# A 16-slot hand-written schedule: first products taken inside the gelu blocks, softplus behind the second one

## What is computed

```python
x = x + 0.5 * ffn(layernorm(x))       # "f1": 8 experts, all computed, the gate's argmax picks one per token
x = x + mamba(layernorm(x))           # rmsnorm, in_proj, conv of 4 taps, silu, scan, gate, out_proj
x = x + 0.5 * ffn(layernorm(x))       # "f2"
# ffn:   h = gelu(x @ W1[e] + b1[e]) (exact gelu);  y = h @ W2[e] + b2[e]
# mamba: dt = softplus(dt_x @ dt_proj_w.T + dt_proj_b)
#        h = exp(dt * A) * h + (dt * x) * B;  y = sum_n h * C + D * x;  256 channels, 16 states each
```

## Time and profile before

| | us |
|---|---|
| median of 3 runs (1549.31 to 1573.08) | 1550.01 |
| the profiled execution, its own time | 1555.03 |
| its span, first to last instruction | 1553.2 |
| mean granted TensorE clock in it | 0.837 of 2.4 GHz |

### The profile page before, as it was taken

One profiled execution on the slowest core, in us unless ns is written; L12 is line 12 of the kernel. 1 busy time (PEld: TensorE's weight loads), 2 busy tenths in 40 slices (PEclk: granted clock), 3 DMA queues, 4 the chain that ended last, 5 costly groups with the idle time before them and its releaser, 6 DMA issues.

```text
span 1553.2 us, 16302 instructions
## 1 busy us (share of the span) xinstructions
PE 1254.8 (81%) x5188; PEld 613.9 (40%) x5188; DVE 1060.3 (68%) x1713; ACT 872.8 (56%) x1171; POOL 1066.0 (69%) x900
## 2 busy tenths in 40 slices
PE   3776858698988988898888988898888878767676
PEld 1333414244343434344343434344343435333343
DVE  2022878868777776768777776778777777979810
ACT  0245655574756657574756557574756566464422
POOL 1026788978586777778586777778586777988500
PEclk9978878798788879888888889898888888888776
DMA  3005141404032322214132322204132322232000
GB/s 81 1 0 198 38 161 42 157 28 161 25 118 79 117 89 103 89 26 173 29 121 76 118 88 91 101 26 173 26 115 78 113 86 104 95 110 88 5 3 14
DMA packets 60405, 130.02 MB, mean 84 GB/s; under 512 B 7744, under 2 KB 26864, under 8 KB 52128
## 3 DMA queue, kind: packets, MB, share of 16 engines
q1 hardware_dynamic: 60320, 128.98, 24.5%
HBM read 106.94 MB, written 22.02 MB: 83 GB/s over the span
## 4 chain that ended last, share of the span: by engine, by line
PE 42%; ACT 31%; DVE 16%; issue 7%; POOL 2%; SPq 1%; ACTq 0%; DMA 0%; DVEq 0%; POOLq 0%
PE PH L451 15%; PE G L440 8%; ACT dA L611 8%; PE PY L466 7%; ACT hs L592 7%; DVE dA L737 6%; PE PH L450 4%; ACT hs L585 4%; DVE hb L735 3%; PE G L520 3%; ACT L592 3%; DVE hb L741 3%; PE Y L478 3%; ACT L593 3%; DVE xs L754 2%
## 5 line engine op out<-in xcount | busy, mean ns | idle before, releaser
L914 POOL TENSOR_TENSOR hb<-dtx_rep,bs 128x1024 f32<-128x1024 f32 x256 | 597.6, 2355 | 0.0
L737 DVE TENSOR_TENSOR_SCAN dA<-dA,hb 128x512 f32<-128x512 f32 x352 | 429.5, 1220 | 62.3 <-ACT dA L611 55.5
L611 ACT ACTIVATE dA<-dt_rep,A 128x512 f32<-128x512 f32 x512 | 338.8, 688 | 147.8 <-DVE hb L741 138.3
L585 ACT COPY hs<-PH 128x512 f32<-128x512 f32 x256 | 149.5, 584 | 431.9 <-PE PH L451 431.6
L451 PE MATMUL PH<-xnT,W 128*128 128x512 f32 x512 | 360.9, 794 | 0.0
L466 PE MATMUL PY<-W,hs 128*128 128x128 f32 x2048 | 325.9, 308 | 0.0
L466 PEld LDWEIGHTS PY<-W,hs 128*128 128x128 f32 x2048 | 282.8, 211 | 100.0 <-issue 88.1
L922 POOL TENSOR_TENSOR hb<-hb,cs 128x1024 f32<-128x1024 f32 x80 | 188.3, 2354 | 186.5 <-DVE hb L735 186.5
L735 DVE TENSOR_TENSOR_SCAN hb<-dA,hb 128x512 f32<-128x512 f32 x160 | 186.9, 1210 | 150.1 <-ACT dA L611 146.1
L741 DVE TENSOR_TENSOR hb<-dA,cs 128x512 f32<-128x512 f32 x352 | 243.5, 692 | 25.2 <-DVE dA L737 0.9
L478 PE MATMUL Y<-hb,Sel 128*32 128x512 f32 x1024 | 168.4, 733 | 16.0 <-DVE hb L741 8.6
(11 more groups left out here) (85 smaller groups left out, 1171.5 us busy)
## 6 DMA issues: line engine op xcount, KB each, us to landing
dtx_rep<-dtx_rows SPq DMA_DIRECT2D x32, 1024.0 KB, 6.6
dt_rep<-dt_rows SPq DMA_DIRECT2D x32, 1024.0 KB, 7.6
bs<-bc_rows SPq DMA_DIRECT2D x64, 256.0 KB, 3.7
...
```

The source lines that it names most:

```text
L585: nc.scalar.copy(hs[:, w, e, :], PH[:, :]).then_inc(ph_free, 1)
L611: nc.scalar.activation(dA[u % NA][:, :], dt_rep[:, h, g, :], ACT.Exp, scale=A[:, h, g, q:q + 1]).then_inc(decay, 1)
L737: nc.vector.tensor_tensor_scan(a, a, x_in_hb, 0.0, ALU.mult, ALU.add).then_inc(scan, 1)
L914: nc.gpsimd.tensor_tensor(hb[:, s % HR], dtx_rep[:, h, 2 * m:2 * m + 2, :], bs[:, q, None, :].broadcast_to([P, 2, CH]), ALU.mult).then_inc ...
```

## The change

Of f2's eight first products, experts 0, 1 and 2 move from slots 1, 2 and 3 of a lap to slot 15 of the lap before; the other five stand in slots 1, 2, 3, 5, 6. f1's experts 0 and 1 stand at the ends of slots 8 and 9 instead of in 9 and 10. A first product and its copy now have places of their own: ACT copies f1's expert 0 between the two gelus of f2's block (slot 7.5), and f2's expert 2 between the two gelus of f1's block (slot 15.5); the copies of slot 15 stand one ahead of the first and one between the two decays. f2's last two second products stand between those first products. softplus moves on ACT from slot 7 to 9.5, behind f2's gelu block and the copy of ln_f2; on POOL dt moves from 8.0 to 9.5 and dt*x from 8.5 to 10.0, and SP's stores of both and its first two fetches from slot 9 to 11. The last sum of the scan moves from slot 1 to slot 0, the output projection and DVE's addition of it one place and one slot earlier, f2's statistics from 6.0 to 5.0, and `gate_f2` behind the first product of slot 10.

```diff
-W1_AT = [[(s, k, 3) for s, k in ((9, 0), (10, 0), (11, 0), (12, 0), (12, 1), (13, 0), (14, 0), (15, 0))],
+W1_AT = [[(8, 2, 7, 3, 3), (9, 2, 9, 0, 3), *[(s, 0, s, 0, 3) for s in (10, 11, 12, 13, 14, 15)]],
...
-ACT_AT = {"ln_f1": 1.5, "silu": 4.0, "bc": 6.0, "dt1": 6.5, "dt0": 7.0, "soft": 7.0, "gelu_f2": 7.5,
+ACT_AT = {"ln_f1": 1.5, "silu": 4.0, "bc": 6.0, "dt1": 6.5, "dt0": 7.0, "soft": 9.5, "gelu_f2": 7.5,
...
-POOL_AT = {"root_f2": 6.5, "norm_f2": 7.0, "dt": 8.0, "dtx": 8.5, "root_p": 11.0, "norm_p": 12.0, "root_f1": 12.5,
+POOL_AT = {"root_f2": 6.5, "norm_f2": 7.0, "dt": 9.5, "dtx": 10.0, "root_p": 11.0, "norm_p": 12.0, "root_f1": 12.5,
...
-                    if s == 1 and it.has(-1):
+                    if s == 0 and it.has(-1):
                         sum_states(it, -1, 7)
...
-                    for unit in w2_units(s):
-                        second_product(it, *unit)
-                    for unit in w1_units(s, 1):
-                        first_product(it, *unit)
+                    for k in (1, 2, 3):
+                        for unit in w1_units(s, k):
+                            first_product(it, *unit)
+                        for unit in w2_units(s, k):
+                            second_product(it, *unit)
...
-            def gelus(it, w):
-
-                it.wait_unit(act, ph_free, w, E - 1, 1)
+            def take_units(it, s, k):
+                for unit in w1_takes(s, k):
+                    take_first(it, *unit)
+
+            def gelus(it, w, s, off):
+
+                if it.has(off):
+                    it.wait_unit(act, ph_free, w, E - 1, 1)
                 for k in range(2):
-                    a = hs[:, w, 4 * k:4 * (k + 1)].rearrange("p e t -> p (e t)")
-                    nc.scalar.activation(a, a, ACT.Gelu).then_inc(gelu[w], 1)
-                nc.scalar.preload_act_table_set(EXP_LN)
+                    if it.has(off):
+                        a = hs[:, w, 4 * k:4 * (k + 1)].rearrange("p e t -> p (e t)")
+                        nc.scalar.activation(a, a, ACT.Gelu).then_inc(gelu[w], 1)
+                    if k == 0:
+                        take_units(it, s, 3)
+                if it.has(off):
+                    nc.scalar.preload_act_table_set(EXP_LN)
...
                 for s in range(SLOTS):
                     stages(it, s)
-                    for unit in w1_units(s, 0):
-                        take_first(it, *unit)
                     off, t = (s + LEAD_X) // SLOTS, (s + LEAD_X) % SLOTS
+                    take_units(it, s, 0)
                     if it.has(off):
-                        decays(it, off, t)
-                    for unit in w1_units(s, 1):
-                        take_first(it, *unit)
+                        make_decay(it, off, 2 * t)
+                    take_units(it, s, 1)
+                    if it.has(off):
+                        make_decay(it, off, 2 * t + 1)
+                    take_units(it, s, 2)
                     stages(it, s + 0.5)
```

More of the change, by code:

```diff
@@ L54 @@
 G_AT = {name: (bank, off) for name, bank, off in G_SEQ}
[L56 removed]
+ACT_AT = {"ln_f1": 1.5, "silu": 4.0, "bc": 6.0, "dt1": 6.5, "dt0": 7.0, "soft": 9.5, "gelu_f2": 7.5,
           "ln_f2": 9.5, "ln_p": 13.5, "taps": 14.5, "gelu_f1": 15.5}
[L58 removed]
+DVE_AT = {"gated1": 1.5, "y_f2": 1.5, "gate_f1": 3.0, "out": 4.5, "oh_f1": 6.0, "stats_f2": 5.0, "gated0": 9.5,
           "y_f1": 10.0, "stats_p": 10.5, "gate_f2": 11.0, "stats_f1": 12.0, "oh_f2": 13.0, "tap01": 15.0, "tap2": 15.5}
[L60 removed]
+POOL_AT = {"root_f2": 6.5, "norm_f2": 7.0, "dt": 9.5, "dtx": 10.0, "root_p": 11.0, "norm_p": 12.0, "root_f1": 12.5,
            "norm_f1": 13.0}
[L62 removed]
+SP_AT = {"x_out": 3, "x_in": 4, "bc": 6, "b0": 8, "dt": 11, "b1": 10, "c0": 10, "b2": 12, "c1": 12, "b3": 14, "dtx1": 14,
          "c2": 14, "dt1": 15, "c3": 15}
[L66 to L69 removed]
+W1_AT = [[(8, 2, 7, 3, 3), (9, 2, 9, 0, 3), *[(s, 0, s, 0, 3) for s in (10, 11, 12, 13, 14, 15)]],
+         [(15, 1, 15, 0, -1), (15, 2, 15, 1, -1), (15, 3, 15, 3, -1), (1, 0, 0, 0, -2), (2, 0, 2, 0, -2),
+          (3, 0, 3, 0, -2), (5, 0, 4, 2, -2), (6, 0, 6, 0, -2)]]
+W2_AT = [[(s, 1, 2) for s in (4, 6, 8, 8, 8, 9, 9, 9)],
+         [(s, k, -2) for s, k in ((10, 1), (11, 1), (12, 1), (13, 1), (14, 1), (14, 1), (15, 1), (15, 2))]]
+W1_ORDER = sorted((s, k, w, e, off) for w in range(2) for e, (s, k, _, _, off) in enumerate(W1_AT[w]))
+W1_TAKES = sorted((s, k, w, e, off) for w in range(2) for e, (_, _, s, k, off) in enumerate(W1_AT[w]))
 W1_PLACE = {(w, e): n for n, (_, _, w, e, _) in enumerate(W1_ORDER)}
@@ L83, in w1_units, with w1_takes, w2_units @@
     return [(w, e, off) for at, k, w, e, off in W1_ORDER if (at, k) == (s, place)]
-def w2_units(s):
-    return [(w, e, off) for w in range(2) for e, (at, off) in enumerate(W2_AT[w]) if at == s]
+def w1_takes(s, place):
+    return [(w, e, off) for at, k, w, e, off in W1_TAKES if (at, k) == (s, place)]
+def w2_units(s, place):
+    return [(w, e, off) for w in range(2) for e, (at, k, off) in enumerate(W2_AT[w]) if (at, k) == (s, place)]
 def g_uses(i, name):
@@ L446, in first_product @@
                 if e == 0:
-                    made = it if w == 0 else it.before()
+                    made = it if off == LN_OFF[w] else it.before()
                     made.wait_read(pe, g_free, f"oh_f{w + 1}")
@@ L585, in take_first @@
                 nc.scalar.copy(hs[:, w, e, :], PH[:, :]).then_inc(ph_free, 1)
-            def gelus(it, w):
-                it.wait_unit(act, ph_free, w, E - 1, 1)
-                for k in range(2):
-                    a = hs[:, w, 4 * k:4 * (k + 1)].rearrange("p e t -> p (e t)")
-                    nc.scalar.activation(a, a, ACT.Gelu).then_inc(gelu[w], 1)
-                nc.scalar.preload_act_table_set(EXP_LN)
[L595 to L612, removed]
@@ new lines, in make_decay @@
+            def make_decay(it, off, u):
+                s = u // 2
+                h, q, m = place(s)
+                g = 2 * m + u % 2
+                if s % 8 == 0 and u % 2 == 0:
+                    it.wait(act, dt_in[h], off, 16, 16)
+                last = [v for v in range(u) if v % NA == u % NA]
+                if last:
+                    back, v = 0, last[-1]
+                else:
+                    back, v = 1, [v for v in range(UN) if v % NA == u % NA][-1]
+                if v // 2 in POOL_C:
+                    it.wait(act, scan, off - back, UN, v + 1)
+                else:
+                    it.wait(act, prod, off - back, NV, on_dve(v + 1))
+                nc.scalar.activation(dA[u % NA][:, :], dt_rep[:, h, g, :], ACT.Exp,
+                                     scale=A[:, h, g, q:q + 1]).then_inc(decay, 1)
@@ L655, in stages @@
                     nc.scalar.activation(sp[:, :, :], sp[:, :, :], ACT.Ln, bias=1.0).then_inc(soft, 1)
[L656 to L659, removed]
+                if t == ACT_AT["gelu_f2"]:
+                    gelus(it, 1, int(t), -2)
+                if t == ACT_AT["gelu_f1"]:
+                    gelus(it, 0, int(t), 3)
             def body(it):
```

## The result

The changed kernel takes 1562.8 us (median of 20 runs), the kernel before 1552.6 (20 runs, beside them): a ratio of 1.0079, with 95% interval 1.0063 to 1.0094. It is slower by 0.8%, which is less than the 2% that the prediction called the bound of a measurement, and still outside the interval of no change. The forecast was 1546, in a range of 1513 to 1578 that holds the result.

A forecast was written before the change was run, and what follows sets the result against it. A chain across engines was taken to bound the kernel, no engine being full. Profiled 1555 us, less 24 over eleven laps (-2.2 each), plus 19 outside them, gave 1550; by the median 1546 us, range 1513 to 1578.

The forecast's parts named there:

- Part c: From the start of f1's gelu block to the end of dt0 on PE: 2.7 us shorter a lap, bounds 1.2 and 4.7.
- DVE's earlier addition of `out` takes away a wait of 0.7 us of PE: In f1's block: a PE wait of 0.7 us goes, counted towards the lap's gain of 3.1 us.
- The half clock: In f1's block: PE's clock falls to half from about 833 until near 843, as before the change.
- rival 1: The clock holds in f1's block: 4.7 us gained there instead of 2.7, 1522 us or 1513; chance 0.15.
- Part a: From dt0's end to PE's sum of slots 8 and 9: 25.9 us, 0.2 longer, with PE waiting 7 us for POOL.
- rival 3: POOL's product is in time for PE's sum, 7 us sooner in eleven laps: 1454 us or about 1470; chance 0.03.
- Part b: From PE's sum to the next f1 gelu block: 0.3 us longer a lap, bounds -0.5 and +3.1.
- rival 2: Half clock stays 14 us after PE's new wait for POOL: 1577 us, or 1595 if f1's block recovers as slowly; chance 0.14.
- My 5 us: Behind PE's wait for POOL's product: half clock lasts 5 us from the sum's start, as in lap 0.
- Start and end: Laps -1, 0 and 1: 5.0, 7.1 and 7.9 us longer; lap 14 and the end: about -1 us.
- it took 5 us more than the median of the runs: Last step, from profiled execution to the median: 1550 us becomes 1546 us.
- The signs: PE's sums wait 7 us a lap for POOL, laps 85.4 us, ACT's wait for first products much the same.

The follow-up runs named there:

- experiment 3: The changed kernel with the output projection's matmuls (`out`) back behind slot 4's second products: 1542.92 us, 0.9937 of the kernel before.
- experiment 10: experiment 6 with f2's first products all back in slots 1 to 7, none in slot 15: 1514.22 us, 0.9758 of the kernel before.
- experiment 6: The changed kernel with softplus, dt and dt*x back at their old places and `out` back behind slot 4's second products: 1476.32 us, 0.9503.
- experiment 1: The changed kernel with softplus, dt, dt*x and their stores back at their old places: 1495.16 us, 0.9629 of the kernel before.
- experiment 8: experiment 6 with f1's first products back at their old places: 1474.02 us, 0.9495 of the kernel before.

## Why the prediction was wrong

**What bounds the kernel.** Right: a chain across engines. The laps, cut in c, a and b, the start and the end account for the difference of the two profiled runs.

**Part c, the step that failed.** Forecast -2.7 us a lap, measured -1.5. The step was "DVE's earlier addition of `out` takes away a wait of 0.7 us of PE": I followed the earlier place of `out` to the engine that takes its result and never asked what `out` itself must wait for. It writes the bank that silu has yet to read, and waits up to 3.6 us, 27.3 us in 14 waits (0.9 in 2 before), where four pairs of second products had stood between. The wait that I meant to take away did go: PE waited 13.4 us in 14 waits for DVE's addition before, and none is left. But it is gone in experiment 3 too, so it is DVE's earlier place alone that takes it away, and the earlier place of `out` on PE, a term that I had put at nothing, only costs. Experiment 3 shows it: with that place undone the wait is 4.0 us, c is 33.2, and the kernel 20 us faster. So without it c gains 3.5, more than I allowed, and `out` took 2 a lap of it. How much of the 3.5 the first products give no run tells; with softplus in front they are worth 1.6 of c a lap (36.14 in experiment 10, 34.54 in experiment 6). That experiment 3's lap, 85.45, is the forecast 85.4 is luck: c gained 0.8 more than forecast and b lost 0.6 more.

The rest of c came as walked. I had forecast gaps of 1.1, 2.1 and 1.7 us; they were 1.18, 2.27 and 0.48. The half clock came as forecast; here is the granted clock (after POOL's busy time) in f1's block of lap 8, and further down in f2's:

```profile
844.00:846.00 2.00, 0.00 (x0) 0.00 (x0) 0.00 (x0) 1.97 (x3) 1.44 (x1) 0.72 0.00 0
846.00:848.00 2.00, 1.82 (x3) 0.60 (x3) 1.25 (x2) 1.94 (x4) 0.00 (x0) 0.50 0.03 8
...
854.00:856.00 2.00, 2.00 (x10) 0.17 (x9) 1.62 (x8) 0.50 (x2) 2.00 (x1) 0.72 0.00 0
...
886.00:888.00 2.00, 1.44 (x3) 0.39 (x3) 2.00 (x4) 2.00 (x5) 0.00 (x0) 1.00 0.00 0
888.00:890.00 2.00, 1.88 (x12) 1.57 (x12) 1.90 (x4) 1.97 (x3) 0.00 (x0) 0.81 0.00 0
890.00:892.00 2.00, 2.00 (x8) 1.28 (x7) 1.97 (x4) 1.78 (x4) 1.82 (x1) 0.50 0.01 4
...
902.00:904.00 2.00, 2.00 (x14) 1.54 (x14) 1.62 (x3) 0.00 (x0) 1.85 (x5) 0.78 0.98 347
```

By these rows it fell at 844.9, 1 us into the second gap, and was at half until 855.2: the ten us that I took over from the earlier trace rows, a little later. That rules out rival 1. The Trainium skill (TensorE: Matmul & The Clock Gate, "Why this matters for your kernels") has only a long idle gap costing the clock; the rows above speak against it for this kernel, at 2.27 us and less.

**Part a.** The time was nearly right (+0.4 for +0.2) and so was its cause: softplus 16.1 us behind dt0 (forecast 16.3), POOL 9.6 us from there to the product (9.5), the sum right behind it. What was wrong is how long PE waits: 4.45 us and not 7. I had PE at the sum 18.8 us behind dt0's end, at full clock throughout; the clock fell at 889.2, and PE was done 21.4 us behind the reading of dt0. Under POOL's product this error hides, and that part a came out right in spite of it is luck. It mis-sized rival 3: experiment 1, the product in time, gave 1495, not 1454 to 1470. Part a is then 22.2 to 23.5, because PE itself is that slow.

**Part b.** Forecast +0.3, measured 0.0. The 0.0 is a mean of two kinds of laps. In lap 8 PE does the sum at half clock after its wait of 4.45 us and is back at full clock at 902.9, 3 us on. So it is in seven of the eleven laps: half clock for 3.0 to 3.7 us behind the start of the sum, b 24.8. In laps 4, 6, 9 and 11 it lasts 9.2 to 9.7 us, and b is 26.6 to 26.8. Lap 4 shows it, with the stretch in which the clock returns:

```profile
552.27 1.94 PE L489 MATMUL Y<-hb,Sel 128*32 128x512 f32 x8 [4.06 <-POOL hb L944]
...
557.22 2.08 PE L462 MATMUL PH<-xnT,W 128*128 128x512 f32 x2
...
560.00:562.00 2.00, 2.00 (x10) 1.48 (x9) 1.30 (x2) 1.17 (x2) 1.90 (x6) 0.61 1.15 356
```

So rival 2, the half clock staying for 14 us, did not come, but a piece of it did, in four laps at 1.8 us each, and the other seven, whose b is 0.6 shorter than the mean before, hide it. My 5 us fit neither kind.

**Start and end.** Forecast +20 and -1, measured +20.5 and -3.2. The sum is nearly right, its reasons less so: softplus in front again takes 12 of the 20 away (experiment 1), and `out` back on top of that 10 more (experiment 6). With softplus late, `out` alone gives nothing there (319.93 in experiment 3): two delays seem to lie side by side, of which I had seen one. By laps, f1's block in lap 0 begins 7.8 us late (forecast 5.0), lap 0 takes 4.8 longer (7.1) and lap 1 7.8 (7.9): the sum is right by errors that cancel.

**The sum.** Eleven laps gave 11.6 instead of 24 (+12.4), the end took 2.2 less than forecast and the start 0.5 more: the profiled run at 1560.8 where 1550 was forecast. The other 6 us are the step "it took 5 us more than the median of the runs", which I subtracted (1550 less 5 is 1545, not the 1546 that I wrote): over 20 runs that run lies 2.4 above the median, and the profiled run after lies 2.0 below its own. Here the offset of one run did not carry over to the other kernel.

**The signs.** Most came. PE's waits were shorter than forecast and the laps longer, and ACT's wait for first products, "much the same" in the forecast, grew by 56 us.

**What the change is made of.** Against the changed kernel: softplus in front again 67 us, `out` behind slot 4's second products 20 us, both 86. Inside what gains: gate_f2 behind slot 10's first product 22 to 24 us, f2's three products in slot 15 38 us, f1's two early ones nothing (5.6 us gained in the laps, 6.3 lost at the start). From 1552.6 to experiment 6 are 76 us; if the parts add, some 14 of them (DVE's and the second products' places, the last sum's) no run took apart. So a forecast of small gains and small losses, near zero in sum, was made over parts that are each worth 20 to 70 us and nearly cancel. Experiments 6 and 8 are the fastest here, 5% under the kernel before.
